# Attention on one core: the weighing of each half of the heads stands directly behind the next scores

## The chip, the cores and the metric

The kernel runs on one core of a Trainium2 chip. The metric is the device time of one execution in microseconds (us). The kernel before was timed three times: 1479.82, 1477.34 and 1478.16 us, median 1478.16.

## The reference

The program computes a small vision tower in float32 for 32 batches of 129 rows with 1024 columns. Three stages follow each other: a state space mixing that makes 128 rows per batch (a class row is put ahead of them), causal attention with 32 query heads on 8 key heads, and a linear layer with values quantised to 8 bits. The attention is what the change touches:

```python
h = h + _L0_attn_ref(_layernorm(h, axis=-1), Wq, Wk, Wv, Wo)

q = (x @ Wq.T) ; k = (x @ Wk.T) ; v = (x @ Wv.T)      # 1024, 256, 256 columns
q = q * cos + _rotate_half(q) * sin                    # the same for k
scores = jnp.einsum('bhgtd,bhkd->bhgtk', qg, k) / math.sqrt(DH)
scores = jnp.where(causal[None, None, None], scores, jnp.finfo(jnp.float32).min)
attn = jax.nn.softmax(scores, axis=-1)
ctx = jnp.einsum('bhgtk,bhkd->bhgtd', attn, v)
return ctx.reshape(...) @ Wo.T
```

## The kernel before

The attention stage takes one batch (a *tile* `t`) per turn of a loop. A turn has `STEPS` = 8 steps `s`. All five engines run the same sequence of turns, each with its own list of work per step, written out by hand in a function `body(t)`; nothing but semaphores ties them together. The turns up to 3 and from 30 on are written out, turns 4 to 29 run in a hardware loop of two turns.

Several batches are under way in one turn. With `t` the batch whose rows are projected, `b` = t-1, `c` = t-2 and `n` = t+1:

- PE (TensorE) projects the rows of `t` on 1536 columns (`project`, L1100): 72 matmuls of 512 columns, nine in each step, in three parts (`w_hi`·`xT_hi`, `w_lo`·`xT_hi`, `w_hi`·`xT_lo`). Short pieces of other work are set between them. Each step issues four projection matmuls, then the pieces, then the other five; `scores` and `turn_k` come ahead of the four.
- Those pieces are: `turn_q(b, 0)` in step 0 and `turn_q(b, 1)` in step 3 (L1124, four transposes of the rotated queries); `scores(b, 0)` in step 1 and `scores(b, 1)` in step 5 (L1145, 16 products that the trace shows as 32 matmuls, on tiles of 32 rows); `turn_k(t)` in step 5 (L1111); `turn_x(n, 0)` and `turn_x(n, 1)` in step 6 (L1134, transposes of the next batch's normalised rows); and `weigh(c, 0)` in step 3 and `weigh(c, 1)` in step 7 (L1159, 16 products of probabilities and values, again 32 matmuls, on tiles of 32 columns).
- ACT (ScalarE) copies what PE leaves in PSUM: queries (`store_q`, L1223), keys (L1217), values (L1249), the upper part of the next rows (`split_x`, L1237) and the weighed half (`context`, L1256). It also makes the exponentials of one group of four heads per step (L1231). Its list is strictly in order: `split_x(n, 0)` in step 6, then that step's exponentials, `split_x(n, 1)` and exponentials in step 7, `context(c, 1)`, and `store_q(b, 0)` at the start of the next turn.
- DVE (VectorE) adds the causal mask (L1400), takes the row maximum (L1409), transposes the normalised probabilities in blocks of 32 (`part_turned`, L1393), subtracts the upper part of the next rows (L1357) and rotates queries and keys (L1378 to L1382).
- POOL (GpSimd) divides the probabilities by their sum (L981), adds the rotated parts (L959), normalises the next rows (L967) and copies single columns aside (`save_ctx` L986, `save_q` L992).
- SP issues DMAs. `part_p` (L876) writes the four blocks of a group's probabilities to a DRAM tensor `p_dram`; `whole_p` (L886) reads the group back, turned, into `pT`, from which `weigh` takes it. `store` (L844) writes a weighed half.

The PSUM bank that `weigh` writes (`C_BANK`) is also the one in which `turn_x(n, 1)` leaves its transposes, and there is a single `pT`, a single `qT` and a single `pB` pair. What guards them are waits on `weighed`, `ctx_ready`, `x_lo`, `q_saved` and `p_parted`.

Of the kernel before, what the change touches and what calls it, by code (L numbers as in the profile page):

```python
# [34 lines left out]
P = 128  # L35
# [64 lines left out]
def shifted(tile, k):  # L100

    m, p = tile
    q = p + k
    return m + q // 2, q % 2
# [12 lines left out]
def fixed(tile):  # L117
    return isinstance(tile[0], int)
# [6 lines left out]
def exists(tile, count):  # L125

    return not fixed(tile) or 0 <= number(tile) < count
# [541 lines left out]
def attention_stage(nc, ctx, cls, h_dram, p_dram, ctx_dram, tail_dram, ml_dram, v0_dram, scale_dram, sbuf, psum, small_sb, cst,  # L669
# [92 lines left out]
    def group_at(t, s, lag):  # L762

        return (shifted(t, -1), s - lag) if s >= lag else (shifted(t, -2), s - lag + STEPS)

    def rounds_at(t, s):

        if at(t, -2):
            return {1: range(8, 12), 2: range(12, 14), 5: range(14, 16), 7: range(16, 18)}.get(s, ())
        if at(t, -1) and s < 4:  # L770
            return range(18 + 2 * s, 20 + 2 * s)
        return ()
# [68 lines left out]
    def sync(sp, load_ahead):  # L841
# [22 lines left out]
        def no_later_keys():  # L864

            sp.wait_ge(c_end_zero, 1)
            for k, q in ((2, 0), (3, 0), (3, 1)):
                sp.dma_start(p_dram[:, DH * k:DH * (k + 1), q, :].rearrange("g k f -> k g f"),
                             c_end[DH * k:DH * (k + 1)]).then_inc(no_keys, 16)

        def part_p(b, g):

            sp.wait_ge(p_turned, STEPS * number(b) + g + 1)
            for q in range(4):
                keys = min(q + 2, 4)
                sp.dma_start(p_dram[g].rearrange("(k d) q f -> q d k f", k=4)[q, :, 0:keys],  # L876
                             pB[DH * q:DH * (q + 1), g % 2, 0:keys].rearrange("d k h f -> d k (h f)")
                             ).then_inc(p_parted[g % 2], 16)

        def whole_p(b, g):  # L880

            if at(b, 0) and g == 0:
                sp.wait_ge(quantised, EC)
                sp.wait_ge(no_keys, 48)
            sp.wait_ge(p_parted[g % 2], 256 * number(b) + 64 * (g // 2) + 64)
            sp.dma_start(pT[:, g // 4, g % 4, :], p_dram[g].rearrange("k q f -> k (q f)")  # L886
                         ).then_inc(p_whole[g // 4], 16)

        def body(t):
            c = shifted(t, -2)  # L890
            if exists(shifted(t, 2), NB) and fixed(t) and number(t) <= 0:
# [26 lines left out]
            for s in range(STEPS):  # L918
                if s == 4 and exists(c, NB):
                    store(c, 0)  # L920
                d, g = group_at(t, s, 4)
                if exists(d, NB):
                    part_p(d, g)
                d, g = group_at(t, s, 5)
                if exists(d, NB):
                    whole_p(d, g)
                if s == 1 and exists(c, NB):
                    store_ml(c)
                if s == 0 and exists(shifted(t, -3), NB):
                    store(shifted(t, -3), 1)  # L930
                if s == 7 and at(t, NB + 1):
                    store(c, 1)
                if at(t, NB) or at(t, NB + 1):
                    load_ahead(sp, number(t) - NB, s)
# [5 lines left out]
    def gpsimd(pool, lower_ahead):  # L940
# [43 lines left out]
        def save_ctx(b, half):  # L984
            pool.wait_ge(ctx_ready, 2 * number(b) + half + 1)
            G.tensor_copy(c_end[:, GQ * half:GQ * half + GQ, bass.ds(number(b), 1)],  # L986
                          ctxo[:, half, :].rearrange("p (q k) -> p q k", q=GQ)[:, :, P - 1:P]
                          ).then_inc(ctx_saved, 1)
# [6 lines left out]
        def body(t):  # L995
# [10 lines left out]
            for s in range(STEPS):  # L1006
# [21 lines left out]
                if s == 4 and has_rows(t):  # L1028
                    rope_sum(t, 0)
                if s == 4 and exists(c, NB):  # L1030
                    save_ctx(c, 0)
                if s == 1 and exists(b, NB):
                    save_q(b, 0)
# [4 lines left out]
                if s == 7 and has_rows(t):  # L1038
                    rope_sum(t, 1)
                if s == 7 and exists(c, NB) and not at(c, NB - 1):  # L1040
                    save_ctx(c, 1)
# [28 lines left out]
    def tensor(pe, turn_wo, project_ahead):  # L1070
# [94 lines left out]
        def body(t):  # L1165
# [4 lines left out]
            for s in range(STEPS):  # L1170
                if s % 4 == 1 and exists(b, NB):
                    scores(b, s // 4)
                if s == 5 and exists(t, NB):
                    turn_k(t)
# [4 lines left out]
                if s == 3 and exists(b, NB):  # L1179
                    turn_q(b, 1)  # L1180
                if s == 3 and exists(c, NB):
                    weigh(c, 0)
# [11 lines left out]
                if s == 6 and has_rows(n) and x_steps(n)[1] is None:  # L1194
                    turn_x(n, 1)
                if s == 7 and exists(c, NB):
                    weigh(c, 1)
# [16 lines left out]
    def scalar(act, copy_wo, upper_ahead, load_wo, load_first):  # L1214
# [56 lines left out]
        def body(t):  # L1271
            b, c, n = shifted(t, -1), shifted(t, -2), shifted(t, 1)
            for s in range(STEPS):
# [9 lines left out]
                if s == 3 and exists(b, NB):  # L1283
                    store_q(b, 1)
                if s == 3 and exists(c, NB):
                    context(c, 0)
# [17 lines left out]
                if exists(d, NB):  # L1304
                    exponentials(d, g)
                if s == 7 and exists(c, NB):
                    context(c, 1)
# [732 lines left out]
def program(nc, x, cls_tok, log_dt, B, inv_A, A_im, Wq, Wk, Wv, Wo, w, bias, consts, out):  # L2040
    h_dram = nc.dram_tensor("h_rows", (NB + 1, P, L), F32, kind="Internal").ap()
    ctx_dram = nc.dram_tensor("ctx_turned", (NB, P, L), F32, kind="Internal").ap()
    p_dram = nc.dram_tensor("p_blocks", (HKV, P, 4, P), F32, kind="Internal").ap()
    tail_dram = nc.dram_tensor("ctx_last_rows", (P, L), F32, kind="Internal").ap()
# [121 lines left out]
```

## Time and profile before

| | |
|---|---|
| median of three runs | 1478.16 us |
| profiled execution, its own time | 1476.76 us |
| its span | 1475.0 us |
| PE busy | 1418.8 us (96%) |
| DVE busy | 1162.4 us (79%) |
| POOL busy | 920.2 us (62%) |
| ACT busy | 725.4 us (49%) |

The profile is of one execution. *Busy* is the time in which an engine runs an instruction; the PE rows overlap (a matmul of 0.39 us starts every 0.23 us), so a start is a better guide on PE than a length. PE fills the span, and granted clock is full in nearly every slice. The attention loop lies roughly between 290 and 960 us of the span.

In the timelines a row is: start in us, length in us, engine, line of the kernel, operation, output <- input, shapes, and how many instructions were merged in it (for merged ones the length is from the first start to the last end). In square brackets stands the engine's idle time just before it and what ended it. A row of waits is: who waited, for whom, us in total, times, longest.

### The profile page before, as it was taken

What the parts mean: (1) busy time and instruction counts of PE and PEld (TensorE: products, weight loads), DVE (VectorE), ACT (ScalarE), POOL (GpSimd) and SP (SyncE); (2) the same over time, 40 slices, a digit from 0 to 9 for tenths busy, and PEclk for the clock granted to TensorE, in tenths of its full rate; (3) what the DMA queues carried; (4) which work ended last, traced back from release to release, by engine and by line L of the source; (5) the groups of instructions that cost most, each with busy time, mean ns of one, the idle gap of its engine ahead of it and who ended that gap; (6) DMA issues with size and microseconds to landing.
All of it is one profiled execution on the core that took longest, in us unless ns stands there. A gap on an engine that the chain in (4) does not pass through costs nothing.

```text
span 1475.0 us, 34108 instructions
## 1 busy us (share of the span) xinstructions
PE 1418.8 (96%) x10442; PEld 1109.0 (75%) x10442; DVE 1162.4 (79%) x2285; ACT 725.4 (49%) x2673; POOL 920.2 (62%) x958
## 2 busy tenths in 40 slices
PE   5999989999999999999999999899999999999997
PEld 3999867777777777777777777676677777777774
DVE  7988678899999999999999999787665555656555
ACT  6897566676767667676767667561000000000000
POOL 5796147676676767676676767445555646555552
PEclk8999999999999999999999999999999999999999
DMA  9356666677777777777777776968444434344441
GB/s 240 102 143 147 191 149 164 191 195 211 204 202 211 202 212 196 208 204 203 203 203 211 205 210 186 284 184 215 134 121 128 135 114 137 115 146 117 132 121 54
DMA packets 264458, 255.60 MB, mean 173 GB/s; under 512 B 73329, under 2 KB 201586, under 8 KB 264402
## 3 DMA queue, kind: packets, MB, share of 16 engines
q1 hardware_dynamic: 257586, 233.87, 57.4%
q10 hardware_dynamic: 6816, 21.04, 4.7%
q8 instruction: 29, 0.48, 0.1%
q14 instruction: 27, 0.22, 0.1%
HBM read 138.26 MB, written 106.57 MB: 166 GB/s over the span
## 4 chain that ended last, share of the span: by engine, by line
PE 72%; DVE 8%; POOL 6%; DMA 4%; SPq 4%; issue 3%; ACT 2%; ACTq 0%; DVEq 0%; POOLq 0%
PE att_ps L1100 30%; PE ffn_o L1757 21%; PE ffn_y L1849 7%; PE att_ps L1145 4%; PE att_ps L1159 3%; POOL yb L358 3%; SPq L876 3%; DMA p_blocks<-pB 2%; PE att_ps L1124 2%; POOL yb L364 2%; PE att_ps L1134 2%; PE mix_ps L447 1%; DMA xqT<-xq 1%; DVE sm L1400 1%; DVE pB L1393 1%
## 5 line engine op out<-in xcount | busy, mean ns | idle before, releaser
L1231 ACT ACTIVATE pr<-sm,ml 128x128 f32<-128x128 f32 x1024 | 399.2, 392 | 223.5 <-DVE ml L1409 222.9
L981 POOL TENSOR_TENSOR pr<-pr,ri 128x512 f32<-128x512 f32 x256 | 265.8, 1043 | 134.8 <-DVE ri L1416 127.6
L1100 PE MATMUL att_ps<-w_hi,xT_hi 128*128 128x512 f32 x776 | 318.9, 411 | 2.6 <-DVE xT_lo L1357 2.0
L1100 PE MATMUL att_ps<-w_lo,xT_hi 128*128 128x512 f32 x776 | 316.5, 408 | 0.0
L1100 PE MATMUL att_ps<-w_hi,xT_lo 128*128 128x512 f32 x776 | 307.2, 396 | 0.0
L1757 PE MATMUL ffn_o<-wo_hi,cT_hi 128*128 128x512 f32 x528 | 211.9, 401 | 1.4 <-ACT wo_hi L1795 1.4
L1811 ACT CAST cT_hi<-ctx_in 128x512 fp32r<-128x512 f32 x64 | 36.4, 616 | 353.9 <-PE ffn_o L1757 350.1
L1757 PE MATMUL ffn_o<-wo_hi,cT_lo 128*128 128x512 f32 x528 | 205.7, 390 | 0.0
L1757 PE MATMUL ffn_o<-wo_lo,cT_hi 128*128 128x512 f32 x528 | 205.4, 389 | 0.0
L1393 DVE STREAM_TRANSPOSE pB<-pr 128x512 f32<-128x512 f32 x256 | 177.7, 694 | 32.3 <-DMA p_blocks<-pB 18.7
L1231 ACT ACTIVATION_READ_ACCUMULATOR pr<-sm,ml 128x1 f32 x1024 | 193.2, 189 | 0.0
L1400 DVE TENSOR_TENSOR sm<-att_ps,cst 128x512 f32<-128x512 f32 x256 | 169.0, 660 | 19.7 <-PE att_ps L1145 19.7
L1409 DVE TENSOR_REDUCE ml<-sm 128x4 f32<-128x512 f32 x256 | 176.2, 688 | 9.1
L1100 PEld LDWEIGHTS att_ps<-w_hi,xT_hi 128*128 128x128 f32 x776 | 146.6, 189 | 43.7 <-issue 8.1
L1100 PEld LDWEIGHTS att_ps<-w_lo,xT_hi 128*128 128x128 f32 x776 | 146.9, 189 | 30.6 <-issue 5.9
L1100 PEld LDWEIGHTS att_ps<-w_hi,xT_lo 128*128 128x128 f32 x776 | 146.6, 189 | 30.3
L1894 DVE TENSOR_TENSOR h<-ffn_o,h_in 128x512 f32<-128x512 f32 x66 | 45.5, 690 | 147.8 <-PE ffn_o L1757 147.7
L1730 POOL TENSOR_TENSOR hb<-h,bias_sb 128x512 f32<-128x512 f32 x66 | 85.5, 1295 | 95.0 <-DVE xq L1935 60.6
L967 POOL TENSOR_SCALAR xn<-hbuf,mv,rstd 128x512 f32<-128x512 f32 x64 | 133.4, 2084 | 0.2
L1849 PE MATMUL ffn_y<-wq,xqT 128*128 128x512 bf16 x528 | 122.6, 386 | 11.3 <-DMA xqT<-xq 11.3
L1757 PEld LDWEIGHTS ffn_o<-wo_hi,cT_hi 128*128 128x128 f32 x528 | 99.2, 188 | 25.3 <-ACT wo_hi L1795 1.8
L447 PE MATMUL mix_ps<-eb,m 128*128 128x128 f32 x1024 | 116.0, 275 | 0.8 <-DVE m L632 0.6
(212 smaller groups left out, 2338.7 us busy)
## 6 DMA issues: line engine op xcount, KB each, us to landing
pT<-p_blocks SPq DMA_DIRECT2D x256, 256.0 KB, 2.9
p_blocks<-pB SPq DMA_DIRECT2D x512, 64.0 KB, 2.0
h_rows<-ho SPq DMA_DIRECT2D x64, 256.0 KB, 3.7
ctx_turned<-ctxo SPq DMA_DIRECT2D x64, 256.0 KB, 3.2
h_in<-h_rows SPq DMA_DIRECT2D x32, 512.0 KB, 3.8
out_dram<-yo SPq DMA_DIRECT2D x32, 512.0 KB, 2.7
ctx_in<-ctx_turned SPq DMA_DIRECT2D x30, 512.0 KB, 3.3
hbuf<-h_rows ACTq DMA_DIRECT2D x29, 512.0 KB, 4.0
```

Source lines behind the costliest of these rows:

```text
L447: mm = nc.tensor.matmul(bank[:, cols], term[:, half, h, slots].rearrange("p j c -> p (j c)"), eb[:, k % 3, half * CH + h, :], start=term i ...
L967: G.tensor_scalar(xn[:, cols], hbuf[:, n[1], cols], mv[:, 0:1], rstd[:], ALU.subtract, ALU.mult).then_inc(xn_ready, 1)
L981: G.tensor_tensor(pr[:, g % 4], pr[:, g % 4], ri[:, g % 2, :].unsqueeze(2).to_broadcast([P, GQ, P]), ALU.mult).then_inc(p_ready, 1)
L1100: mm = nc.tensor.matmul(bank[:], x_part[:, t[1], e, tok:tok + P], w_part[blk][:, e, :], start=(r == 0), stop=(r == EC * 3 - 1))
L1145: mm = nc.tensor.matmul(S_BANK[j][:, q * P:(q + 1) * P], qT[rows, half, q, :], kT[rows, b[1], half, :], start=True, stop=True)
L1231: a = nc.scalar.activation(pr[:, g % 4, q, :], sm[:, g % 2, q, :], ACT.Exp, bias=ml[:, b[1], 0, h:h + 1], accum_out=ml[:, b[1], 1, h:h + 1])
L1393: V.transpose(pB[:, g % 2].rearrange("p k h f -> p h k f"), pr[:, g % 4].rearrange("p h (k f) -> p h k f", k=4)).then_inc(p_turned, 1)
L1400: V.tensor_tensor(sm[:, g % 2], S_BANK[g % 4][:].rearrange("p (q k) -> p q k", q=GQ), cst[:, C_MASK:C_MASK + P].unsqueeze(1).to_broadcast( ...
L1409: V.tensor_reduce(ml[:, b[1], 0, heads_of(g)], sm[:, g % 2], AX.X, ALU.max, negate=True).then_inc(negmax_ready, 1)
L1730: done = nc.gpsimd.tensor_tensor(hb[:, t[1], cols], h1[:, t[1], cols], bias_sb[:, cols], ALU.add)
L1757: mm = nc.tensor.matmul(O_BANK[half][:], c_part[:, t[1], e, :], w_part[:, e, half * BK:(half + 1) * BK], start=(r == 0), stop=(r == PER_HA ...
L1849: mm = nc.tensor.matmul(Y_BANK[half][:], xqT[:, c[1], e, :], wq8[:, e, half * BK:(half + 1) * BK], start=(e == 0), stop=(e == EC - 1))
```

## The change

Seven things are changed, all in the order of work:

1. `weigh(c, 0)` goes from step 3 to step 5, directly behind `scores(b, 1)` and ahead of `turn_k(t)`. `weigh(c, 1)` goes from step 7 to step 1 of the next turn, directly behind `scores(b, 0)` of that turn. This holds for the turns before the last (`weighed_late`).
2. ACT's `context` copies follow: step 3 to step 5 (ahead of `store_k` and the exponentials), step 7 to step 1 of the next turn (ahead of the exponentials).
3. POOL's `save_ctx` follow: step 4 to 6, step 7 to step 2 of the next turn.
4. SP's `store` of the weighed halves: step 4 to 6, step 0 to 2.
5. `whole_p` is issued one step later, six steps behind the scores of its group instead of five, except for the last two batches.
6. `p_dram` has two copies, one for odd and one for even batches; the zero blocks are written in both.
7. `part_p` gets two waits on `weighed`, ahead of its fourth DMA of groups 2 and 6, which keep `whole_p` from overwriting a half of `pT` that is still being weighed.

The diff, shortened to its core:

```diff
+    def weighed_late(t):
+        return not (fixed(t) and number(t) >= NB - 1)
...
         def part_p(b, g):
             sp.wait_ge(p_turned, STEPS * number(b) + g + 1)
             for q in range(4):
+                if q == 3 and g == 2:
+                    at_least(sp, weighed, 2 * number(b) - 1)
+                if q == 3 and g == 6:
+                    at_least(sp, weighed, 2 * number(b))
                 keys = min(q + 2, 4)
-                sp.dma_start(p_dram[g].rearrange("(k d) q f -> q d k f", k=4)[q, :, 0:keys],
+                sp.dma_start(p_dram[b[1], g].rearrange("(k d) q f -> q d k f", k=4)[q, :, 0:keys],
...
# SP, body
-                if s == 4 and exists(c, NB):
+                if s == 4 and not weighed_late(t) and exists(c, NB):
                     store(c, 0)
...
+                d, g = group_at(t, s, 6)
+                if exists(d, NB) and not (fixed(d) and number(d) >= NB - 2):
+                    whole_p(d, g)
                 d, g = group_at(t, s, 5)
-                if exists(d, NB):
+                if exists(d, NB) and fixed(d) and number(d) >= NB - 2:
                     whole_p(d, g)
...
# POOL, body
-                if s == 4 and exists(c, NB):
+                if s == (6 if weighed_late(t) else 4) and exists(c, NB):
                     save_ctx(c, 0)
+                if s == 2 and weighed_late(b) and exists(shifted(t, -3), NB):
+                    save_ctx(shifted(t, -3), 1)
...
# PE, body
                 if s % 4 == 1 and exists(b, NB):
                     scores(b, s // 4)
+                if s == 1 and weighed_late(b) and exists(shifted(t, -3), NB):
+                    weigh(shifted(t, -3), 1)
+                if s == 5 and weighed_late(t) and exists(c, NB):
+                    weigh(c, 0)
                 if s == 5 and exists(t, NB):
                     turn_k(t)
...
-                if s == 3 and exists(c, NB):
+                if s == 3 and not weighed_late(t) and exists(c, NB):
                     weigh(c, 0)
...
-                if s == 7 and exists(c, NB):
+                if s == 7 and not weighed_late(t) and exists(c, NB):
                     weigh(c, 1)
...
# ACT, body
-                if s == 3 and exists(c, NB):
+                if s == 1 and weighed_late(b) and exists(shifted(t, -3), NB):
+                    context(shifted(t, -3), 1)
+                if s == (5 if weighed_late(t) else 3) and exists(c, NB):
                     context(c, 0)
...
-    p_dram = nc.dram_tensor("p_blocks", (HKV, P, 4, P), F32, kind="Internal").ap()
+    p_dram = nc.dram_tensor("p_blocks", (2, HKV, P, 4, P), F32, kind="Internal").ap()
```

How the order changes on PE, from `turn_q(b, 1)` (`cst,rsq`) in step 3 to `turn_k` (`cst,rsk`) in step 5 of one turn; `pT,v_sb` is the weighing and `kT,qT` the scores. Before:

```order
L1124 MATMUL att_ps<-cst,rsq 128x128 x4
L1159 MATMUL att_ps<-pT,v_sb 32x128 x16
L1100 MATMUL att_ps<-w_lo,xT_hi 128x512
...
L1100 MATMUL att_ps<-w_hi,xT_lo 128x512
L1145 MATMUL att_ps<-kT,qT 128x128 x16
L1111 MATMUL att_ps<-cst,rsk 128x128 x2
L1100 MATMUL att_ps<-w_hi,xT_hi 128x512
```

And now, the same stretch:

```order
L1140 MATMUL att_ps<-cst,rsq 128x128 x4
L1116 MATMUL att_ps<-w_lo,xT_hi 128x512
...
L1116 MATMUL att_ps<-w_hi,xT_lo 128x512
L1161 MATMUL att_ps<-kT,qT 128x128 x16
L1175 MATMUL att_ps<-pT,v_sb 32x128 x16
L1127 MATMUL att_ps<-cst,rsk 128x128 x2
L1116 MATMUL att_ps<-w_hi,xT_hi 128x512
```

The weighing of half 0 has moved from behind `turn_q(b, 1)` to between the scores and the transposes of the keys; the one of half 1 leaves the end of the turn in the same way and stands behind the next turn's first scores.

On ACT, from `split_x(n, 0)` in step 6 to the copy of the queries at the start of the next turn (`pr,ml` are exponentials, `ctxo` the weighed half). Before:

```order
L1237 CAST xT_hi<-att_ps 128x4x128
L1231 ACTIVATE pr,ml<-sm,ml 128x128 x4
L1237 CAST xT_hi<-att_ps 128x4x128
L1231 ACTIVATE pr,ml<-sm,ml 128x128 x4
L1256 COPY ctxo<-att_ps 128x512
L1223 COPY qT<-att_ps 128x512
```

And now:

```order
L1257 CAST xT_hi<-att_ps 128x4x128
L1251 ACTIVATE pr,ml<-sm,ml 128x128 x4
L1257 CAST xT_hi<-att_ps 128x4x128
L1251 ACTIVATE pr,ml<-sm,ml 128x128 x4
L1243 COPY qT<-att_ps 128x512
```

One copy has left this stretch; the rest of it is in the same order. The order on DVE is the same before and after.

## Rows read from the trace of the kernel before

**Rows 1.** Busy time of each engine, 400 to 900 us: PE, PEld, DVE, ACT, POOL.
```profile
400.00:900.00 500.00, 500.00 (x4592) 393.74 (x4591) 465.58 (x1014) 347.34 (x1522) 357.54 (x401) 1.00 0.74 205
```

**Rows 2.** Waits, 400 to 900 us.
```profile
POOL c_end L986 <- ACT ctxo L1256: 72.7, 21, 3.7
PEld att_ps L1145 <- ACT qT L1223: 7.7, 21, 0.4
```

**Rows 3.** Timeline of PE, steps 5 and 6: second scores, keys, first transposes of rows.
```profile
702.52 1.17 PE L1145 MATMUL att_ps<-kT,qT 32*128 32x128 f32 x32
703.62 0.44 PE L1111 MATMUL att_ps<-cst,rsk 128*128 128x128 f32 x2
703.82 0.47 PE L1100 MATMUL att_ps<-w_hi,xT_hi 128*128 128x512 f32 x1
...
706.94 0.60 PE L1134 MATMUL att_ps<-cst,xn 128*128 128x128 f32 x4
```

**Rows 4.** Timeline of PE, end of step 7 to step 1: weighing, queries, first scores.
```profile
710.83 0.40 PE L1100 MATMUL att_ps<-w_hi,xT_lo 128*128 128x512 f32 x1
711.16 1.08 PE L1159 MATMUL att_ps<-pT,v_sb 128*32 128x128 f32 x32
...
712.51 0.39 PE L1100 MATMUL att_ps<-w_lo,xT_hi 128*128 128x512 f32 x1
...
713.20 0.60 PE L1124 MATMUL att_ps<-cst,rsq 128*128 128x128 f32 x4
713.55 0.48 PE L1100 MATMUL att_ps<-w_lo,xT_hi 128*128 128x512 f32 x1
...
714.91 1.17 PE L1145 MATMUL att_ps<-kT,qT 32*128 32x128 f32 x32
```

**Rows 5.** Timeline of ACT over the same stretch.
```profile
707.57 0.59 ACT L1237 CAST xT_hi<-att_ps 128x512 fp32r<-128x512 f32 x1 [0.71 <-PE att_ps L1134]
...
709.61 0.57 ACT L1237 CAST xT_hi<-att_ps 128x512 fp32r<-128x512 f32 x1
712.25 0.41 ACT L1231 ACTIVATE pr<-sm,ml 128x128 f32<-128x128 f32 x1 [2.08 <-DVE ml L1409]
...
713.81 0.57 ACT L1256 COPY ctxo<-att_ps 128x512 f32<-128x512 f32 x1
714.28 0.58 ACT L1223 COPY qT<-att_ps 128x512 f32<-128x512 f32 x1
```

**Rows 6.** Timeline of ACT, one turn later.
```profile
737.94 0.58 ACT L1223 COPY qT<-att_ps 128x512 f32<-128x512 f32 x1
```

**Rows 7.** Timeline of PE, one turn later.
```profile
738.58 1.17 PE L1145 MATMUL att_ps<-kT,qT 32*128 32x128 f32 x32
```

**Rows 8.** Timeline of DVE, steps 7 and 4.
```profile
710.21 0.69 DVE L1357 TENSOR_TENSOR xT_lo<-att_ps,xT_hi 128x512 fp32r<-128x512 f32 x1 [0.54 <-ACT xT_hi L1237]
...
725.11 0.65 DVE L1400 TENSOR_TENSOR sm<-att_ps,cst 128x512 f32<-128x512 f32 x1
```

**Rows 9.** Timeline of PE, steps 3 to 5: queries, weighing, second scores.
```profile
721.23 0.60 PE L1124 MATMUL att_ps<-cst,rsq 128*128 128x128 f32 x4
721.76 1.08 PE L1159 MATMUL att_ps<-pT,v_sb 128*32 128x128 f32 x32
722.77 0.50 PE L1100 MATMUL att_ps<-w_lo,xT_hi 128*128 128x512 f32 x1
...
726.19 1.17 PE L1145 MATMUL att_ps<-kT,qT 32*128 32x128 f32 x32
```

**Rows 10.** All instructions of line L1145: duration ns min/median/max, first and last start.
```profile
L1145 PE MATMUL att_ps<-kT,qT x2048: 270/270/373, 213.2 to 982.3; 32*128 32x128 f32 x187
```

**Rows 11.** Timeline of SP: DMA issues of steps 6 and 1.
```profile
706.60 1.79 SPq L876 DMA_DIRECT2D p_blocks<-pB  x4
...
718.73 0.38 SPq L886 DMA_DIRECT2D pT<-p_blocks  x1
```

**Rows 12.** DMA issues of the page: KB each, us to landing.
```profile
pT<-p_blocks SPq DMA_DIRECT2D x256, 256.0 KB, 2.9
```

More of the change, by code:

```diff
@@ L866, in no_later_keys @@
             sp.wait_ge(c_end_zero, 1)
-            for k, q in ((2, 0), (3, 0), (3, 1)):
-                sp.dma_start(p_dram[:, DH * k:DH * (k + 1), q, :].rearrange("g k f -> k g f"),
-                             c_end[DH * k:DH * (k + 1)]).then_inc(no_keys, 16)
+            for copy in range(2):
+                for k, q in ((2, 0), (3, 0), (3, 1)):
+                    sp.dma_start(p_dram[copy, :, DH * k:DH * (k + 1), q, :].rearrange("g k f -> k g f"),
+                                 c_end[DH * k:DH * (k + 1)]).then_inc(no_keys, 16)
         def part_p(b, g):
@@ L883, in whole_p @@
                 sp.wait_ge(quantised, EC)
-                sp.wait_ge(no_keys, 48)
+                sp.wait_ge(no_keys, 96)
             sp.wait_ge(p_parted[g % 2], 256 * number(b) + 64 * (g // 2) + 64)
-            sp.dma_start(pT[:, g // 4, g % 4, :], p_dram[g].rearrange("k q f -> k (q f)")
+            sp.dma_start(pT[:, g // 4, g % 4, :], p_dram[b[1], g].rearrange("k q f -> k (q f)")
                          ).then_inc(p_whole[g // 4], 16)
         def body(t):
-            c = shifted(t, -2)
+            b, c = shifted(t, -1), shifted(t, -2)
             if exists(shifted(t, 2), NB) and fixed(t) and number(t) <= 0:
@@ L928, in body @@
                     store_ml(c)
-                if s == 0 and exists(shifted(t, -3), NB):
+                if s == 6 and weighed_late(t) and exists(c, NB):
+                    store(c, 0)
+                if s == (2 if weighed_late(b) else 0) and exists(shifted(t, -3), NB):
                     store(shifted(t, -3), 1)
@@ L1039, in body @@
                     rope_sum(t, 1)
-                if s == 7 and exists(c, NB) and not at(c, NB - 1):
+                if s == 7 and not weighed_late(t) and exists(c, NB) and not at(c, NB - 1):
                     save_ctx(c, 1)
@@ L1305, in body @@
                     exponentials(d, g)
-                if s == 7 and exists(c, NB):
+                if s == 7 and not weighed_late(t) and exists(c, NB):
                     context(c, 1)
```

## The prediction

> **What bounds the kernel now.** I read the busy times of a long stretch of the attention first. PE runs for 500.00 of 500 us, DVE for 465.58, POOL for 357.54 and ACT for 347.34 [rows 1]. So PE sets the time and each microsecond less on PE seems to be one won. The waits are read next, for a PE that is always busy can still be led. One row tells of that: in 21 turns of 21, the weight load of one of the two scores was released by ACT's copy of the queries [rows 2]. Its 7.7 us are no loss by themselves, 0.37 us each, about what every switch of PE to such tiles takes. But they say that the copy comes no sooner than PE asks for it.
>
> The timelines show how exactly. The copy `qT` starts at 714.28 and lasts 0.58, so it ends at 714.86, and the scores start at 714.91 [rows 4, 5]. A turn later it ends at 738.52 and the scores start at 738.58 [rows 6, 7]. One turn is 738.58 - 714.91 = 23.67 us. PE and this copy arrive together, and there is no slack between them that I can see.
>
> What leads to that copy is a chain of fixed lengths that starts with `turn_x(n, 0)` on PE at 706.94 [rows 3]: the first cast of the next rows at 707.57, behind it four exponentials, the second cast at 709.61, DVE's subtraction that waits for this cast [rows 8], mask and maximum on DVE, four exponentials from 712.25 on (ACT had stood still for 2.08 us for them), the copy of the weighed half at 713.81, the copy of the queries [rows 5]. It takes 714.91 - 706.94 = 7.97 us, and PE has work of the same length in that stretch.
>
> **The change part by part.** I cut a turn in three: A from the second scores to `turn_x(n, 0)`, B from there to the first scores of the next turn, C from those to the second scores.
>
> A is 706.94 - 702.52 = 4.42 us of PE work [rows 3]. The weighing of half 0 is put in directly behind the scores. A weighing takes 722.77 - 721.76 = 1.01 us from its start to the next piece [rows 9]. The step from scores to a weighing is not in this trace. Call x what it costs beyond the 1.10 us that scores take up to `turn_k` [rows 3]. A becomes 5.43 + x.
>
> B loses the weighing of half 1 on PE. From 710.83 to 712.51 stand two projections and the weighing, 1.68 us; two projections alone take 0.46, as three of them take 713.20 - 712.51 = 0.69 [rows 4]. So PE's work in B falls by 1.22 to 6.75 us. The chain beside it loses one copy on ACT, 714.28 - 713.81 = 0.47 [rows 5], and no other member: the order on ACT and DVE is otherwise the same there. It becomes 7.50. PE now arrives at the scores 7.50 - 6.75 = 0.75 us too early and waits. B is 7.50, not 6.75. This is the step that decides: the chain starts from `turn_x(n, 0)`, which the change makes later (A), and work that filled PE during the chain is taken out of B.
>
> C is 726.19 - 714.91 = 11.28 us [rows 4, 9]. It gains a weighing behind the scores, 1.01 + x. It loses one behind `turn_q(b, 1)`: from those transposes to the next projection are 722.77 - 721.23 = 1.54 us with it [rows 9] and 713.55 - 713.20 = 0.35 without [rows 4], so 1.19 less. C becomes 11.10 + x.
>
> The turn is then 5.43 + 7.50 + 11.10 + 2x = 24.03 + 2x against 23.67, longer by 0.36 + 2x. PE's own work is shorter by 1.22 + 1.19 - 2.02 = 0.39 less 2x. That is the saving of an excursion, and the 0.75 of waiting is more than it. It is one excursion less and not a halving: leaving the projections happened seven times in a turn and now happens six times, as `turn_q` and `turn_x` stay where they are.
>
> For x: the burst of scores lasts 1.17 us [rows 3], the last of its 32 matmuls 0.27 of it [rows 10], so that one starts at 0.90 and the next piece at 1.10. If the weighing could follow at the burst's own pace (0.90 / 31 = 0.03), it would come 0.17 us sooner: x = -0.17. The other end is a weighing behind transposes, 721.76 - 721.23 = 0.53 [rows 9], where a projection follows after 0.35: x = 0.18. I take 0, by the nearest row: the keys follow the same burst after 1.10, with a change of tiles between them.
>
> That row shows 0.20 us from the start of the last scores matmul to the start of `turn_k`, where the pace of the burst is 0.03 [rows 3, 10]. The Trainium skill (TensorEngine Tiling (Array Packing), Key Properties) says that a change of the tiling mode, not of the tile alone, drains the engine. By it scores (32 rows) and weighing (32 columns) still have a drain between them, so x is 0 or more; without such a rule the sum would go down to the lower end above. No row here has the two side by side.
>
> Edits that I cost at nothing, with what hides them:
> - POOL's `save_ctx`. POOL now stands 72.7 / 21 = 3.46 us per turn waiting for the copy of half 1 [rows 2], with a normalisation queued behind. That wait goes or shrinks. POOL is not in A, B or C; the gain stays on POOL.
> - ACT's copy of half 0 ahead of `store_k` and the exponentials of step 5. The weighing ends 1.10 + 1.08 = 2.18 us after the scores began [rows 3, 9], then the copy 0.57, the keys' copy (below 0.57) and four exponentials, 713.81 - 712.25 = 1.56 [rows 5]. They are over by 4.9. The first cast is due at 5.43 + 0.63 = 6.06. 1.2 us are spare; past that each microsecond would lengthen B.
> - SP's waits on `weighed`. The fourth DMA of group 2 comes at about 706.60 + 1.34 = 707.9 [rows 11], the weighing it waits for ends 2.18 after 702.52, at 704.7. Spare: 3.2 us. Behind it on SP stand `whole_p` and the next groups, for which DVE would wait with `pB`.
> - `whole_p` a step later. That of group 3 now goes out where group 4's did, at 718.73 [rows 11], and lands 2.9 us later [rows 12], at 721.6. The weighing that needs it comes at 726.19 + 1.10 = 727.3. 5.7 us are spare. Only in turn 31, where the weighing of half 0 stays in step 3 (721.76), is it close: 0 to 0.3 us, once.
> - The second copy of `p_dram` adds three DMAs of zeroes once.
>
> How often: the three cuts hold together from turn 2 to turn 30, 29 times. The first turns still carry the preparation of weights and have other waits, so I count 28. 28 x 0.36 = 10.1 us. Against the profiled execution of 1476.76 us this is 1486.8; the median of the runs lies 1.4 us higher, 1478.16, and gives 1488.2. I forecast 1488.2.
>
> **The rivals.**
> - *Faster: the saving arrives.* Were the queries' copy early, PE would take 0.39 less per turn: 28 x 0.39 = 10.9 us, 1467.3. Its place is the first scores of each turn, its price the whole 0.75; it decides once the chain is 6.75 or shorter. For it speaks that PE is never idle [rows 1]. Against it: the 7.50 are made of lengths alone, with PE's own waiting nowhere in them, and the copy already ends just when the scores start [rows 4 to 7]. Chance 0.10.
> - *No change: the drain between scores and weighing falls away.* x = -0.17 gives 0.02 per turn, 0.6 us, 1478.8. The burst's pace speaks for it [rows 10], the 0.20 ahead of the keys against it. Chance 0.08.
> - *DVE takes over in C.* The second scores overwrite the bank of the fourth mask, which ends at 725.11 + 0.65 = 725.76, 15.55 us after the start of DVE's second subtraction at 710.21 [rows 8]. In the new turn this subtraction starts 710.21 - 706.94 = 3.27 into B, so the mask ends 3.27 + 15.55 - 7.50 = 11.32 into C, against 11.10 of PE. If those 15.55 stay whole, with DVE's own waits, PE waits 0.22 more: 28 x 0.58 = 16.2, 1494.4. Against it: POOL's wait [rows 2], which holds up what DVE transposes there, goes. Chance 0.17.
> - *The switch is dear.* x = 0.18 gives 0.72 per turn, 20.2 us, 1498.3. Chance 0.08.
>
> **How the numbers follow.** A measurement of this kernel tells about 0.2% (3.0 us) from no change. The forecast has 0.57. Slower are the forecast and the last two rivals, 0.82, of which I give 0.02 to a value of x that brings it inside 3 us: slower 0.80, same 0.10, faster 0.10. The range goes from 1478 (most of the case without change is in it) to 1500 (the dear switch and 2 us). Outside it are the faster case and a few hundredths at either end.
>
> **What would show it.** Right: PE has idle time of about 0.75 us ahead of the first scores in each turn, released by ACT's copy of the queries, 20 us in all; the copy ends 7.45 us after `turn_x(n, 0)` starts; a turn is 24.0 us; the second scores and the weighing are 1.10 us apart; POOL no longer waits 3.5 us for a weighed half. Wrong: no idle time ahead of those scores, or a turn under 23.67 us. A wait of PE ahead of the second scores, released by DVE's mask, would speak for the third rival, and one of a weighing for `pT` against my account of the DMAs.

## The result and the profile after

The changed kernel takes 1491.38 us (median of 4 runs, 1484.67 to 1495.78) against 1478.38 for the kernel before (4 runs of the same chip): ratio 1.0076, interval 1.0052 to 1.0099, slower by 11.2 us (7.7 to 14.6) by the ratio; the two medians lie 13.0 apart. The profiled execution is the fastest of the four: 1484.67 us, span 1482.9.

The busy times of the same stretch, 400 to 900 us (PE, PEld, DVE, ACT, POOL; then granted clock, DMA share, GB/s), answer to [rows 1]:

```profile
400.00:900.00 500.00, 486.31 (x4554) 389.08 (x4553) 459.07 (x1001) 343.75 (x1497) 352.20 (x397) 1.00 0.74 202
```

Before, PE was busy for 500.00 of 500 us. Now 13.7 are missing, at a granted clock of 1.00 both times. The list of waits of that stretch says whose they are (answers to [rows 2]):

```profile
PEld att_ps L1161 <- ACT qT L1243: 22.8, 21, 1.1
...
PE att_ps L1161 <- ACT qT L1243: 13.7, 21, 0.7
DVE pB L1415 <- DMA p_blocks<-pB: 11.7, 41, 0.4
```

All 13.7 us are one wait, once in each of 21 turns, 0.65 each: the first scores wait for the queries that ACT copies. POOL's 72.7 us for `c_end` [rows 2] have left the list. The timeline of PE gives the cuts A, B and C; both pairs of scores and weighing are in it (answers to [rows 3, 4, 7, 9]):

```profile
703.94 1.17 PE L1161 MATMUL att_ps<-kT,qT 32*128 32x128 f32 x32
705.04 1.08 PE L1175 MATMUL att_ps<-pT,v_sb 128*32 128x128 f32 x32
706.05 0.44 PE L1127 MATMUL att_ps<-cst,rsk 128*128 128x128 f32 x2
...
709.37 0.60 PE L1150 MATMUL att_ps<-cst,xn 128*128 128x128 f32 x4
...
715.78 0.40 PE L1116 MATMUL att_ps<-w_hi,xT_lo 128*128 128x512 f32 x1
716.85 1.17 PE L1161 MATMUL att_ps<-kT,qT 32*128 32x128 f32 x32 [0.67 <-ACT qT L1243]
717.96 1.08 PE L1175 MATMUL att_ps<-pT,v_sb 128*32 128x128 f32 x32
...
727.97 1.17 PE L1161 MATMUL att_ps<-kT,qT 32*128 32x128 f32 x32
```

A is 709.37 - 703.94 = 5.43, B is 716.85 - 709.37 = 7.48, C is 727.97 - 716.85 = 11.12, the turn 24.03. Over turns 7 to 28 the median turn is 24.05 (24.02 to 24.08), before it was 23.70 (23.66 to 23.73). The timeline of ACT in the same turn shows the chain to the copy (answers to [rows 5]):

```profile
710.00 0.59 ACT L1257 CAST xT_hi<-att_ps 128x512 fp32r<-128x512 f32 x1 [1.28 <-PE att_ps L1150]
...
712.04 0.56 ACT L1257 CAST xT_hi<-att_ps 128x512 fp32r<-128x512 f32 x1
714.68 0.40 ACT L1251 ACTIVATE pr<-sm,ml 128x128 f32<-128x128 f32 x1 [2.08 <-DVE ml L1431]
...
716.24 0.56 ACT L1243 COPY qT<-att_ps 128x512 f32<-128x512 f32 x1
```

The copy ends at 716.80 and the scores start at 716.85. The 2.08 us ahead of the exponentials are as long as before.

How far does this carry? From the first scores of turn 7 to those of turn 31 (24 turns) are 577.26 us, before 568.86: 8.4 us, 0.35 a turn. Turn 31 itself, from its first scores to those of turn 32, takes 36.28 against 32.58, another 3.7. There two weighings wait for their probabilities, which none did before, and a third one stands ahead of them: half 1 of batch 28, which the change moved out of turn 30 (PE's timeline; the rest of the turn is left out):

```profile
934.45 1.08 PE L1175 MATMUL att_ps<-pT,v_sb 128*32 128x128 f32 x32
...
942.23 1.08 PE L1175 MATMUL att_ps<-pT,v_sb 128*32 128x128 f32 x32 [0.95 <-DMA pT<-p_blocks]
...
959.16 1.93 PE L1175 MATMUL att_ps<-pT,v_sb 128*32 128x128 f32 x32 [3.77 <-DMA pT<-p_blocks]
963.05 1.12 PE L1140 MATMUL att_ps<-cst,rsq 128*128 128x128 f32 x4 [1.96 <-POOL rsq L973]
```

The first scores of turn 7 start 3.3 us sooner in this profile (356.09 against 359.38), and this differs from profile to profile: 356.1 and 358.0 for the changed kernel, 359.3 to 361.3 for kernels with the weighing of before. Most of it arises from the first scores of turn 2 to those of turn 7: 120.26 us (119.78 in the second profile of the changed kernel) against 122.93, and 124.13 and 125.84 in the two other kernels with the weighing of before. Three things can be read in the turns. Turn 2 has lost a weighing, 1.01 us, the one that turn 31 has gained. In turn 3 of the kernel before, the weighing of half 1 stood 2.14 us for DVE's subtraction, which empties the bank that this weighing writes; no weighing of the changed kernel waits for it. And that turn has a dip of the clock that the changed kernel has not: PE is busy for 25.36 us of it, 23.81 in the turn behind it (PE's timeline and the windows view, before):

```profile
282.51 1.08 PE L1159 MATMUL att_ps<-pT,v_sb 128*32 128x128 f32 x32 [2.14 <-DVE xT_lo L1357]
```

```profile
260.32:287.82 27.50, 25.36 (x218) 19.89 (x218) 23.16 (x52) 17.43 (x77) 18.35 (x21) 0.94 0.68 185
287.82:311.75 23.93, 23.81 (x219) 18.68 (x218) 20.84 (x46) 15.60 (x69) 15.42 (x19) 1.00 0.68 183
```

The clock dips ahead of turn 2 as well. In the windows view, of 120 to 180 and 240 to 300 us (the second holds the dip of turn 3), the kernel before has

```profile
120.00:180.00 60.00, 56.09 (x462) 53.71 (x461) 46.73 (x54) 35.31 (x63) 20.20 (x22) 0.97 0.59 156
...
240.00:300.00 60.00, 57.76 (x527) 45.36 (x529) 52.32 (x118) 39.49 (x174) 41.41 (x49) 0.97 0.68 189
```

and the changed one

```profile
120.00:180.00 60.00, 55.37 (x462) 52.65 (x461) 46.41 (x55) 34.68 (x61) 20.91 (x23) 1.00 0.61 165
...
240.00:300.00 60.00, 58.17 (x543) 46.49 (x543) 53.61 (x121) 41.41 (x184) 44.86 (x50) 1.00 0.73 195
```

A mean of 0.97 over 60 us is 3.6 us at the lower level (1.2 GHz); the kernel before has two such stretches here that the changed one has at 1.00. So I compare kernels by the 24 turns, and use whole times for verdicts alone.

### The profile page after: what moved, and what is told of

The parts are those of the page before. It is cut to its first block, busy times and chain, and to the rows that moved or that the text cites. A ratio compares the mean times of both kernels' runs of the same rounds, so it can differ in the third digit from the quotient of the medians.

```text
span 1482.9 us, 34189 instructions
## 1 busy us (share of the span) xinstructions
PE 1403.7 (95%) x10442; PEld 1106.4 (75%) x10442; DVE 1160.6 (78%) x2285; ACT 727.4 (49%) x2673; POOL 919.3 (62%) x958
## 4 chain that ended last, share of the span: by engine, by line
PE 62%; DVE 11%; ACT 7%; POOL 6%; issue 5%; DMA 5%; SPq 3%; ACTq 1%; DVEq 0%; POOLq 0%
PE ffn_o L1779 21%; PE att_ps L1116 21%; PE ffn_y L1871 7%; ACT pr L1251 4%; PE att_ps L1161 4%; PE att_ps L1175 3%; POOL yb L358 3%; DMA p_blocks<-pB 2%; DVE sm L1422 2%; SPq L885 2%; POOL yb L364 2%; DVE ml L1431 2%; PE mix_ps L447 1%; ACT xT_hi L1257 1%; PE att_ps L1150 1%
```

## The experiments

The theory after the result: the turn is a ring from `turn_x(n, 0)` over ACT, DVE and ACT to the first scores (B), and over PE back to `turn_x` (C and A); the change lengthened its PE part by one weighing and shortened the other by one copy. Rivals were a cost of the DMA edits, DVE's ring in C, and a cost of the switch from scores to weighing.

### The changed kernel again

No edit.

> The changed kernel once more, for the spread of its times and a second profile. Theory (the chain of ACT and DVE to the copy of the queries sets the turn): every turn of the loop 24.05 us, PE idle 0.65 us ahead of each first scores, as in its first profile; in turn 31 PE waits about 4.7 us for pT again; the times lie around 1491 us and what they differ by stands ahead of turn 6 or behind turn 30, not in the loop. Rival (the DMAs of the probabilities hold the turn up, from run to run by another amount): the turns themselves differ between the two profiles.

Measured: 1487.77 us (6 runs), ratio 1.0061 (1.0042 to 1.0079). The turn is 24.05, the wait ahead of the first scores 0.63 to 0.68, the 24 turns 577.29, turn 31 takes 37.64, with waits for `pT` of 1.09 and 6.21. The loop repeats to 0.03 us; turn 31 differs by 1.4.

### SP's edits alone

The DMA edits of the change (two copies of `p_dram`, the waits on `weighed`, `whole_p` a step later) in the kernel before; both weighings stay where they were.

```diff
 # before, SP's edits of the change only
+                if q == 3 and g == 2:
+                    at_least(sp, weighed, 2 * number(b) - 1)
...
+                d, g = group_at(t, s, 6)
+                if exists(d, NB) and not (fixed(d) and number(d) >= NB - 2):
+                    whole_p(d, g)
```

> Of the change only what is SP's: two copies of the blocks in DRAM, the probabilities fetched a step later, the two waits on the weighing. PE, ACT, POOL as in the kernel before. Theory: the turn stays 23.70 us; the weighing of half 0 in step 3 has its pT just in time (0 to 0.1 us of wait), and turn 31 takes 3.7 us more, since its weighings still stand in steps 3 and 7: 1478 to 1484 us. Rival (the DMAs carry the loss): 23.9 us and more per turn, 1490.

Measured: 1482.43 us (12 runs), ratio 1.0019 (1.0002 to 1.0037). The turn stays 23.70, the 24 turns are 569.06 against 568.86, PE is busy for 500.00 of 500. The edit costs nothing in the loop. Turn 31 takes 35.06 against 32.58, 2.5 more, where I had expected the whole 3.7. PE's timeline has two new waits in it:

```profile
937.96 1.08 PE L1171 MATMUL att_ps<-pT,v_sb 128*32 128x128 f32 x32 [2.64 <-DMA pT<-p_blocks]
953.11 1.15 PE L1171 MATMUL att_ps<-pT,v_sb 128*32 128x128 f32 x32 [2.81 <-DMA pT<-p_blocks]
```

2.5 us of turn 31 and 2.8 us (0.3 to 5.5) of the whole are SP's edits. The loop's 8.4 are not. The 1.2 us of turn 31 that are left are about the one weighing more that it has in the changed kernel, 1.01.

### Each half alone

```diff
 # half 0 alone: half 1 is weighed in step 7 as before
-                if s == 1 and weighed_late(b) and exists(shifted(t, -3), NB):
-                    weigh(shifted(t, -3), 1)
...
-                if s == 7 and not weighed_late(t) and exists(c, NB):
+                if s == 7 and exists(c, NB):
                     weigh(c, 1)
```

```diff
 # half 1 alone: half 0 is weighed in step 3 as before
-                if s == 5 and weighed_late(t) and exists(c, NB):
-                    weigh(c, 0)
...
-                if s == 3 and not weighed_late(t) and exists(c, NB):
+                if s == 3 and exists(c, NB):
                     weigh(c, 0)
```

The copies, `save_ctx`, `store` and fetches of each half go with it.

> The change for half 0 alone: its weighing behind the second scores, half 1 stays at the end of the turn. Theory: A 5.43 us; B stays 7.97 on PE, the chain with its copy of the weighed half 7.95; no wait ahead of the first scores. C would be 10.1 on PE, but the ring over DVE is 5.43 + 3.26 + 15.02 to 15.44 (POOL's wait for the copy of half 1 is still there) + 0.07: turn 23.8 to 24.2 us, with PE waiting for DVE's mask ahead of the second scores; 1485 to 1496 us with the cost of turn 31. Rival (PE's work alone decides): turn 23.49, 6 us less than before, 1472 to 1476. Rival (each half carries half of the loss of the change): turn 23.88 with the wait ahead of the first scores.

> The change for half 1 alone: its weighing behind the next turn's first scores, half 0 stays in step 3; groups of half 0 are fetched as before, those of half 1 a step later. Theory: A 4.42 us; B 7.48, PE idle 0.75 ahead of the first scores; C 12.30. Turn 24.20 us, 0.50 more than before, more than the whole change costs: 28 x 0.50 = 14 us, and 3 us in turn 31: about 1494. Rival (each half carries half of the loss): turn 23.88, 1486. Rival (PE's work alone decides): turn 23.48.

Measured: half 0 alone 1494.14 us (6 runs), ratio 1.0094 (1.0073 to 1.0114), turn 24.32 (24.11 to 24.51), above the 23.8 to 24.2 that I expected; half 1 alone 1494.03 (6 runs), 1.0101 (1.0077 to 1.0126), turn 24.24. Each half alone is worse than both together (24.05). For half 1 alone the ring explains it: from second to first scores are 11.90 = 4.42 + 7.48, that is A as before and B with the same wait for `qT` of 0.65, and C is 12.34, one weighing (1.01) more than 11.31. Half 0 alone is another matter. C is 10.91, and the wait has another releaser, and stands ahead of the second scores (PE's timeline, and two rows of its waits from 400 to 900 us):

```profile
708.65 1.17 PE L1159 MATMUL att_ps<-kT,qT 32*128 32x128 f32 x32 [0.58 <-DVE sm L1416]
```

```profile
POOL c_end L1000 <- ACT ctxo L1272: 97.9, 21, 4.7
...
PE att_ps L1159 <- DVE sm L1416: 14.6, 20, 0.9
```

The mask that the second scores wait for is the one named in the rival "DVE takes over in C". That wait is real, one edit away from the changed kernel.

### The queries copied between the exponentials

If the ring binds by the end of the copy, a copy that overtakes two exponentials should return most of the wait.

```diff
             for q in range(GQ):
+                if q == 2 and t is not None and q_between(t):
+                    store_q(t, 0)
                 h = 16 * (g // 4) + 4 * q + g % 4
```

> The changed kernel, but ACT copies the queries for the first scores between the second and the third of the four exponentials of step 7, not behind them. Theory: the copy then ends at about the time at which PE gets there by itself, the 0.65 us of waiting ahead of the first scores go. But the turn gets shorter by 0.27 us only, to 23.78, since the next ring lies there: second scores to turn_x 5.43, from there to DVE's second subtraction 3.26, DVE's own work up to the fourth mask 15.02, 0.07 to the second scores. PE then waits 0.4 to 0.5 us ahead of the second scores, released by DVE's mask. 28 x 0.27 = 7.6 us less than the changed kernel, 1484. Rival (ACT's copy is the only bound, PE follows): turn 23.31, 1470. Rival (the wait is not ACT's doing): no change.

Measured: 1487.86 us (12 runs), ratio 1.0055 (1.0037 to 1.0073). PE's wait for `qT` is gone, as expected, and the turn falls only to 23.89: PE now waits ahead of the second scores. In its list of waits:

```profile
PEld att_ps L1161 <- ACT qT L1243: 9.3, 21, 0.6
PE att_ps L1161 <- DVE sm L1427: 8.5, 21, 0.4
```

DVE's ring stood right behind ACT's: 24.05 - 23.89 = 0.16 us a turn was all that the copy could give back (I had expected 0.27). The 24 turns are 573.08, 4.2 us less than in the changed kernel; the whole time shows none of it (1487.77 for the changed kernel measured beside it), and in this profile turn 31 took 42.50, with weighings waiting 1.67 and 6.90 us for `pT`.

### `turn_x` sooner

The chain starts from `turn_x(n, 0)`. It needs nothing that PE makes in step 6, so it can go ahead of that step's four projections, and `turn_x(n, 1)` behind them, where the first stood.

```diff
+                early_x = s == 6 and has_rows(n) and x_steps(n)[1] is None
+                if early_x:
+                    turn_x(n, 0)
                 if has_rows(t):
                     project(t, min(s * per_step, count), min(s * per_step + ahead, count))
+                if early_x:
+                    turn_x(n, 1)
```

The same edit was made in the kernel before as a control: there PE has no wait that it could take away.

> The changed kernel, but PE transposes the next rows four projections earlier, both halves (0.93 us). It takes back the delay of turn_x(n, 0) that the weighing behind the second scores brought. Theory: A falls from 5.43 to 4.50 us, PE's own work in B is 7.67 and longer than the chain of 7.48, so no wait ahead of the first scores; C stays 11.12. Turn 23.30 us, 0.75 below the changed kernel and 0.40 below the kernel before: 28 x 0.75 = 21 us less than the changed kernel, about 1470; PE has no idle time in the loop. Rival (DVE is the bound behind it): the ring over DVE is 22.85 and would have to be longer than I read it; then the turn is 23.5 or more with PE waiting for DVE's mask. Rival (switches of PE between tiles cost more with the new neighbours): no faster than 24.05 - 0.4.

> The kernel before, with the same move of the transposes of the next rows (four projections earlier), a control. Theory: in the kernel before PE and the chain arrive together, PE is the bound; an earlier chain gives slack only. Turn 23.70 us, no change, within 2 us of 1478. Rival (the kernel before was itself held by the copy of the queries, the 0.33 us ahead of the scores being partly a wait): the turn falls by up to 0.1 us, 3 us in all. Rival (the transposes are simply better placed there, whatever the weighing does): as much gained here as in the changed kernel, 0.7 us per turn.

Measured: in the changed kernel 1466.84 us (6 runs), ratio 0.9920 (0.9903 to 0.9937). In the kernel before 1475.45 (12 runs), ratio 0.9979 (0.9968 to 0.9989), with the turn at 23.67 (568.16 for 24 turns against 568.86). The control gained about 3 us in its whole time, where I had expected no more than 2 either way, and only 0.7 of them are in the 24 turns; where the rest arises is open. It is small beside the 20.9 us between the changed kernel (1487.77 beside it) and the same with `turn_x` sooner. The changed kernel with it is PE-bound from 400 to 900 us, in the windows view:

```profile
400.00:900.00 500.00, 500.00 (x4683) 401.41 (x4682) 474.16 (x1033) 355.20 (x1546) 362.59 (x409) 1.00 0.75 207
```

PE's and ACT's timelines of a turn show no wait ahead of the scores, and the copy ending at 704.19, 0.24 before them:

```profile
696.75 0.60 PE L1150 MATMUL att_ps<-cst,xn 128*128 128x128 f32 x4
...
704.43 1.17 PE L1161 MATMUL att_ps<-kT,qT 32*128 32x128 f32 x32
```

```profile
703.63 0.56 ACT L1246 COPY qT<-att_ps 128x512 f32<-128x512 f32 x1
```

The turn is 23.30, which is 0.40 under the kernel before: the saving on PE that the prediction worked out as 0.39. The 24 turns are 559.71, 17.6 us less than in the changed kernel, for an edit of order alone. In the kernel before, the same move gave 0.7. This settles what held the change back in the loop.

### The last fetches sooner

The turn-31 waits suggested fetching batch 29's last five groups a step sooner again.

```diff
+        def sooner(d, g):
+            return fixed(d) and (number(d) >= NB - 2 or number(d) == NB - 3 and g >= 3)
...
-                if exists(d, NB) and not (fixed(d) and number(d) >= NB - 2):
+                if exists(d, NB) and not sooner(d, g):
                     whole_p(d, g)
```

With `turn_x` sooner, once by itself and once more side by side, and then in the changed kernel alone:

> The changed kernel with the transposes of the next rows four projections earlier, and in turn 31 the last five groups of batch 29 fetched as early as before. Theory: 23.30 us per turn as without the second edit, and PE's waits for pT in turn 31 (0.95 and 3.77 us in the changed kernel) fall to under 1 us together: 3 to 4 us less than with the first edit alone, about 1467 and 11 us below the kernel before. Rival (those waits are covered or come back later, at the start of the last stage): the same time as with the first edit alone.

> The changed kernel with the transposes of the next rows four projections earlier, once more, beside the version with the edit of turn 31 on the same chip. Theory: 23.30 us per turn and PE waits for pT in turn 31 (0.24 and 7.19 us in its first profile); about 1467 us. Rival (its first profile had an unlucky turn 31): those waits are gone in this profile without the edit.

> The same with the last groups of batch 29 fetched as early as before. Its first times were those of the version without this edit (1466.73 against 1466.84 us), though its profile showed 5 us less between the first scores of turns 31 and 32. Theory: the waits for pT are real work lost and the edit gives 2 to 4 us when both run on one chip. Rival: what PE waits less for pT it waits more for POOL's rotated queries right behind (4.19 us there), nothing is gained, within 1 us.

> The changed kernel with the edit of turn 31 alone. Theory: turn 24.05 us as in the changed kernel; from the first scores of turn 31 to those of turn 32 about 33 to 35 us where it took 36.3 and 37.6; 1485 to 1487 us, 1 to 4 less than the changed kernel. Rival (the wait is only handed on to POOL's queries): as long as the changed kernel, 1488.

| kernel | us (runs) | ratio (interval) | 24 turns | turn 31 |
|---|---|---|---|---|
| `turn_x` sooner | 1466.84 (6) | 0.9920 (0.9903 to 0.9937) | 559.71 | 40.59 |
| `turn_x` sooner, again | 1471.63 (10) | 0.9947 (0.9926 to 0.9968) | 560.35 | 36.42 |
| with the tail edit | 1466.73 (6) | 0.9911 (0.9889 to 0.9933) | 559.28 | 35.30 |
| with the tail edit, again | 1470.10 (6) | 0.9939 (0.9926 to 0.9952) | 559.28 | 39.43 |
| changed kernel, tail edit | 1490.05 (5) | 1.0076 (1.0063 to 1.0089) | 577.72 | 35.80 |

The edit wins nothing that can be told from the spread. In the changed kernel with it, PE's timeline of turn 31 shows why:

```profile
944.20 1.08 PE L1180 MATMUL att_ps<-pT,v_sb 128*32 128x128 f32 x32 [0.52 <-DMA pT<-p_blocks]
...
959.44 1.08 PE L1180 MATMUL att_ps<-pT,v_sb 128*32 128x128 f32 x32 [1.56 <-DMA pT<-p_blocks]
964.66 1.11 PE L1145 MATMUL att_ps<-cst,rsq 128*128 128x128 f32 x4 [4.14 <-POOL rsq L978]
```

The waits for `pT` shrink from 0.95 and 3.77 to 0.52 and 1.56, and PE's next wait, for POOL's rotated queries, grows from 1.96 to 4.14; in the kernel before it was 4.16. The wait was handed on. My theory of what this edit would gain fell.

### Half 0 alone with `turn_x` sooner

```diff
 # half 0 alone, and as above
+                if early_x:
+                    turn_x(n, 0)
```

> The change for half 0 alone, and the transposes of the next rows four projections earlier. Theory of two rings: the ring over DVE, which set half 0 alone to 24.32, is 0.93 shorter, 23.39; PE's own work is 5.43 + 7.97 + 10.11 = 23.51 and becomes the longer one. Turn 23.51 us, no wait in the loop, 0.19 less than the kernel before: 28 x 0.19 = 5 us less, 3 us lost again in turn 31, 1476. Rival (the wait of half 0 alone is POOL's, which stands 4.7 us for the copy of half 1, and not a matter of when turn_x comes): PE goes on waiting for DVE's mask, turn 24 us and more.

Measured: 1487.41 us (6 runs), ratio 1.0051 (1.0035 to 1.0067), turn 24.03, C 10.64: a miss, with the turn that the rival on record had. I had taken DVE's ring to start at its second subtraction and run freely. Its timeline shows it stopping again further on, for the first scores themselves:

```profile
713.95 0.69 DVE L1376 TENSOR_TENSOR xT_lo<-att_ps,xT_hi 128x512 fp32r<-128x512 f32 x1 [0.65 <-ACT xT_hi L1256]
...
719.85 0.71 DVE L1412 STREAM_TRANSPOSE pB<-pr 128x512 f32<-128x512 f32 x1 [0.43 <-POOL pr L995]
720.94 0.69 DVE L1419 TENSOR_TENSOR sm<-att_ps,cst 128x512 f32<-128x512 f32 x1 [0.38 <-PE att_ps L1159]
...
729.35 0.65 DVE L1419 TENSOR_TENSOR sm<-att_ps,cst 128x512 f32<-128x512 f32 x1
```

And its timeline of PE, with the piece from which B is counted:

```profile
706.16 1.17 PE L1159 MATMUL att_ps<-kT,qT 32*128 32x128 f32 x32 [0.47 <-DVE sm L1419]
...
710.67 0.60 PE L1148 MATMUL att_ps<-cst,xn 128*128 128x128 f32 x4
...
719.60 1.17 PE L1159 MATMUL att_ps<-kT,qT 32*128 32x128 f32 x32
...
730.23 1.17 PE L1159 MATMUL att_ps<-kT,qT 32*128 32x128 f32 x32 [0.44 <-DVE sm L1419]
```

The first scores start at 719.60, the mask on them at 720.94, the fourth mask ends at 730.00 and the second scores start at 730.23. DVE has no idle time between that mask and the fourth one. So from first to second scores it needs about 10.64, however soon the rest comes. Half 1 is still weighed in B, where PE waits for nothing: the turn is 4.51 (A) + 8.93 (B) + 10.63 (C) = 24.07. With weighing of half 1 in C, C is 11.12 of PE's own work and this limit is covered. That DVE sets C here is shown by the wait and its releaser; that it is the whole reason for half 0's 24.32 without the edit is argued, since POOL's wait for `c_end` (97.9 us there, 78.5 with the edit) changes with it too.

## Why the prediction was right

- **The step that decides, B.** Predicted 7.50 with a copy ending 7.45 after `turn_x(n, 0)` and a wait of 0.75; measured 7.48, 7.43 and 0.65. The wait's releaser is the one named. The 0.65 counts from the modelled end of the projection before; the turn shows the whole price, 24.05 - 23.30 = 0.75 with `turn_x` sooner. The runs with the copy or `turn_x` sooner remove the wait and leave the DVE wait or none.
- **A and C.** Predicted 5.43 + x and 11.10 + x; measured 5.43 and 11.12.
- **x.** From scores to weighing are 705.04 - 703.94 = 1.10 and 717.96 - 716.85 = 1.11: x is 0.00 to 0.01, not -0.17 and not 0.18. The rule of the Trainium skill (TensorEngine Tiling (Array Packing), Key Properties), that a change of the tiling mode drains the engine, agrees with this: the weighing did not follow at the burst's pace. The cheap and the dear switch are both out.
- **The turn.** Predicted 0.36 longer, measured 0.35. PE's own work was to fall by 0.39; with the wait taken away it fell by 0.40 (23.70 to 23.30).
- **The edits at nothing.** POOL's wait for `c_end` went. ACT waited 1.28 us for the first cast where I had 1.2 spare. SP's edits cost nothing in the loop: 23.70 with them alone, and in the changed kernel no weighing waits for `pT` before turn 31. DVE waits more for its partial DMAs, 11.7 us over 21 turns (2.7 before), off the path.
- **The rival in C** did not bind, and by less than I allowed it: DVE's timeline answers to [rows 8]:

```profile
712.63 0.69 DVE L1379 TENSOR_TENSOR xT_lo<-att_ps,xT_hi 128x512 fp32r<-128x512 f32 x1 [1.26 <-ACT xT_hi L1257]
...
727.00 0.65 DVE L1422 TENSOR_TENSOR sm<-att_ps,cst 128x512 f32<-128x512 f32 x1
```

The mask ends at 727.65, 15.02 after the subtraction started, where the rival carried over 15.55 whole. DVE's wait for POOL in that stretch, 0.42 us before (at 716.10), is gone, as the argument against the rival had it. PE came at 727.97, 0.32 behind the mask; a DVE mask that did release the scores ended 0.23 ahead of them (730.00 and 730.23 above). So little covered it, and the copy between the exponentials and half 0 alone ran into it. The prediction gave this rival 0.17; it stayed covered by 0.1 to 0.2 us a turn.
- **Turn 31, a term that was mis-sized.** I had "0 to 0.3 us, once", for half 0. It was 3.7 and 5.1 in two profiles of the changed kernel (36.28 and 37.64, before 32.58), 2.5 in the one with SP's edits alone. Three things were missing. Half 1 also keeps its place in step 7 of that turn while its last fetch is later. I had used the loop's landing time of 2.9 us [rows 12]; the eight fetches issued from 932 to 960 us landed after 5.4 us (median) in the kernel before already, and after 5.0 in the changed one. And each turn hands a weighing on to the next, so turn 2 has one less and turn 31 one more, 1.01 us each; I had counted neither. The fetch for which PE stood 3.77 us was issued at 954.64 and landed 4.5 us later, when the weighing started (959.16); the row has it together with the next fetch, issued at 957.22, ahead of which SP itself waited 2.1 us:

```profile
954.64 2.92 SPq L895 DMA_DIRECT2D pT<-p_blocks  x2
```
- **The first turns, the other mis-sized term.** "Other waits, so I count 28" left four turns at +0.36 for turns 2 to 6, 1.4 us more. They took 2.7 and 3.2 us less (120.26 and 119.78 against 122.93): the weighing that turn 2 hands on, the wait of 2.14 us gone, and the dip of the clock in the one profile of the kernel before. With SP's edits alone the same turns had no dip and took 124.13, with waits of PE of 2.6 us for DVE's subtraction and 2.3 for `pT`.

The terms from the first scores of turn 2 to those of turn 32 are then -2.7 + 8.4 + 3.7 = 9.4 us in the first profile of the changed kernel and -3.2 + 8.4 + 5.1 = 10.3 in the second, against the one profile of the kernel before. The forecast of 10.1 has one of the three right, the loop's 8.4 (24 x 0.36 = 8.6); that the sum comes out too is luck, since the other two are wrong with opposite signs. The whole times say 11.2 (7.7 to 14.6) and 9.0 (6.2 to 11.7). How much of the -3 is the change and how much the clock of that execution stays open.

## What to carry to other kernels

An engine that is busy for 100% of a stretch may be tied with a chain through other engines: before taking work out of it, find where that chain starts and ends, and which of the pieces moved lie on its two sides. Work taken out beside the chain and put in ahead of its start makes the turn longer, though the sum of work falls. The repair here was to start the chain sooner (two groups of transposes moved by 0.93 us turned +0.35 us a turn into -0.40), and the next ring behind it should be priced at the same time. Price the first and the last turns apart: a piece moved into the next turn leaves the first one and lands in the last, and waits and landing times there are not those of the loop.

## What the runs showed of the hardware that was not expected

- A weighing (128 rows, 32 columns) behind scores (32 rows, 128 columns) starts 1.10 to 1.11 us after them, as the 128 x 128 transposes do, in each timeline read here. Which of the two shapes follows the scores made no difference.
- A fetch of 256 KB into `pT` lands 2.9 us after its issue in the loop (median of 169 from 400 to 900 us, 2.5 to 4.1, kernel before), and 5.4 (2.7 to 6.0) in the eight from 932 to 960 us. In the changed kernel these are 2.9 and 5.0 (up to 7.0), and the waits for them differ between two executions of it by 2.6 us (0.95 and 3.77, then 1.09 and 6.21).
- Where the granted clock dips in the first 300 us differs from execution to execution. The start of turn 7 differs too, by up to 5.1 us for the same kernel (354.85 and 359.98 with `turn_x` sooner; how much of it is the clock is not shown), while 24 turns at full clock repeat within 0.7 us (577.26 and 577.29; 559.71 and 560.35).
